# The rotary stage of a four-layer network on one core: the last two feed-forward batches get banks and buffers of their own, the value projections stand earlier, one output product is cut in two

## What is computed

```
# attention: 16 query heads, 4 key/value heads of 128, 128 context + 128 own keys
q, k, v = x @ wq, x @ wk, x @ wv ;  kc, vc = ctx @ wk_ctx, ctx @ wv_ctx
q, k, kc = rms_norm(q), rms_norm(k), rms_norm(kc);  q, k = rope(q), rope(k)
probs = softmax(q @ concat(kc, k).T / sqrt(128) + causal)     # 128 x 256 per head
x = x + tanh(g) * (probs @ concat(vc, v)) @ wo                # wo: 2048 x 256
# feed-forward with quantised rows (127 levels, per row) and ternary weights, hidden 1024
h = silu(quant(norm(x)) @ gate_w.T + gate_b) * (quant(norm(x)) @ val_w.T + val_b)
x = x + tanh(g') * (quant(h) @ out_w.T + out_b)
```

## Time and profile before

| | us |
|---|---|
| median of 3 runs (lowest, highest) | 2508.88 (2505.51, 2517.94) |
| the profiled execution | 2485.77 |
| its span in the trace | 2483.6 |
| mean granted TensorE clock, share of full | 0.952 |
| busy in the span: TensorE, VectorE, ScalarE, GpSimd | 2174.7, 1512.0, 1125.3, 745.6 |

### The profile page before, as it was taken

The page is one execution under the profiler, slowest core; times in us unless marked ns, Lnnn a source line. Parts: engine busy times, 40 slices in busy tenths (PEclk is TensorE's granted clock), DMA queues, the critical chain, the costliest instruction groups (busy, mean ns, idle before and its releaser), DMA issues. The chain is left out here.

```text
span 2483.6 us, 38366 instructions
## 1 busy us (share of the span) xinstructions
PE 2174.7 (88%) x10438; PEld 1376.0 (55%) x10486; DVE 1512.0 (61%) x3702; ACT 1125.3 (45%) x3555; POOL 745.6 (30%) x932
## 2 busy tenths in 40 slices
PE   6969999988888688879999999999995788869999
PEld 3446677756455344435556656665653444445685
DVE  6975434456455577765676777677765577753244
ACT  2021244411455355545565556555552477742242
POOL 5705500056233200023344444344433100003104
PEclk9969999999999899999999999999997699979999
DMA  6902245453200000000000000000000000201143
GB/s 218 300 21 85 91 136 161 147 163 114 118 1 0 3 1 0 0 26 1 1 1 1 0 0 0 0 0 0 0 0 1 5 5 4 84 24 42 61 134 100
DMA packets 85587, 127.18 MB, mean 51 GB/s; under 512 B 12418, under 2 KB 74626, under 8 KB 84226
## 3 DMA queue, kind: packets, MB, share of 16 engines
q1 hardware_dynamic: 75490, 98.52, 12.5%
q0 software_dynamic: 9984, 27.28, 3.5%
HBM read 91.41 MB, written 47.84 MB: 56 GB/s over the span
## 5 line engine op out<-in xcount | busy, mean ns | idle before, releaser
L2371 ACT ACTIVATE l2x_prob<-l2x_pS,l2x_nb,l2x_rms_q 128x256 f32<-128x256 f32 x256 | 142.5, 565 | 116.5 <-DVE l2x_nb L2606 114.7
L1035 ACT ACTIVATE moe_act_g<-moe_pG 128x96 f32<-128x96 f32 (+1 forms) x159 | 53.2, 335 | 267.2 <-PE moe_pU L968 186.9
L1186 PE MATMUL l2x_pQ<-big,l2x_xT 128*128 128x512 f32 x312 | 149.6, 602 | 4.7 <-DVE l2x_part L2584 4.3
L2603 DVE TENSOR_REDUCE l2x_negmax<-l2x_pS 128x2 f32<-128x512 f32 x128 | 87.7, 685 | 92.5 <-PE l2x_pS L2191 89.7
L928 POOL DMA_INDIRECT moe_yk<-route_y,moe_slot_i x72 | 71.1, 987 | 218.9 <-DMA route_y<-moe_y 188.5
L3113 DVE TENSOR_TENSOR l3f_hid<-l3f_act_g,l3f_pA 128x256 f32<-128x256 f32 (+1 forms) x103 | 38.1, 370 | 159.0 <-ACT l3f_act_g L3024 117.6
L2201 PE MATMUL l2x_pOT<-l2x_probT,l2x_v 128*128 128x512 f32 x256 | 124.7, 610 | 4.5 <-ACT l2x_probT L2386 4.5
L2191 PE MATMUL l2x_pS<-l2x_kT,l2x_qT 128*128 128x256 f32 x512 | 128.3, 380 | 0.0
L2937 PE MATMUL l3f_pA<-big,l3f_xnT 128*128 128x512 f32 x256 | 125.4, 614 | 0.0
L2210 PE MATMUL l2x_pT<-big,l2x_oT 128*128 128x256 f32 x512 | 121.1, 379 | 0.7 <-ACT l2x_oT L2379 0.7
L1515 ACT ACTIVATE l1f_ex<-l1f_pS,l1f_negmax 128x128 f32<-128x128 f32 x256 | 73.0, 368 | 104.0 <-DVE l1f_negmax L1546 104.0
(11 more groups left out here) (498 smaller groups left out, 5753.1 us busy)
## 6 DMA issues: line engine op xcount, KB each, us to landing
route_x<-in_c_zero SPq DMA_DIRECT2D x1, 13184.0 KB, 81.6
moe_xg<-route_x SPq DMA_DIRECT2D x103, 128.0 KB, 2.2
route_y<-moe_y SPq DMA_DIRECT2D x103, 128.0 KB, 1.7
big<-in_e_gu SPq DMA_DIRECT2D x1, 6144.0 KB, 19.0
l3f_xg<-route_x SPq DMA_DIRECT2D x39, 128.0 KB, 2.2
route_y<-l3f_y SPq DMA_DIRECT2D x39, 128.0 KB, 1.7
big<-in_f_gu SPq DMA_DIRECT2D x1, 4096.0 KB, 12.2
big<-in_e_down SPq DMA_DIRECT2D x1, 3072.0 KB, 25.0
```

The lines of the kernel that those rows point to most:

```text
L1186: last = pe.matmul(out, lhsT=xT[:, k, :], rhs=w[:, k, cols], start=(k == 0), stop=(k == KC - 1))
L2371: ins = act.activation(prob[g % 2][:, h, :], pS[j][:, (h % 2) * 2 * P:(h % 2 + 1) * 2 * P], ACT.Exp, scale=rms_q[g][:, h:h + 1], bias=nb[: ...
L2603: dve.tensor_reduce(negmax[:, c], pS[j][:].rearrange("p (h k) -> p h k", h=2), AX.X, ALU.max, negate=True).then_inc(S["max_steps"], 1)
```

## The change

1. TensorE and ScalarE: `value_rows` of x moves from the end of slot 3 (and of the prologue) to slot 0 of its own batch, that of the context from the end of slot 0 to slot 1. Both now stand right behind `proj` (TensorE) and `squares` (ScalarE).
2. TensorE: in slot 3 `output` is cut into heads 0 and 1 before the second `turn_probs`, and heads 2 and 3 behind it.
3. The last batch has its own feed-forward rows, in attention buffers that are free by then (`prob`, `probT`, `qT`, `krows`). The four `f_up` products of the last two batches go to pQ, pTq, pS0, pS1; the turn of x of batch 15 goes to pP, the turn of h and output product of batch 14 to pOT. Their waits follow these buffers.
4. `finish` is written out anew on each engine: the products of batch 14 stand between the last attention steps. The rounding of the hidden rows of batches 14 and 15 goes from GpSimd to ScalarE.

```diff
+        f_rows = (f_gate, f_val, f_th[:], f_xqT[:], f_qh_q[:], f_hqT)
+        f_rows_last = (prob[0][:].rearrange("p h k -> p (h k)"), prob[1][:].rearrange("p h k -> p (h k)"),
+                       probT[:].rearrange("p a h t -> p (a h t)"),
...
+        def up_bank(c, n):
+            return (pQ, pTq, pS[0], pS[1])[n] if is_last(c, 2) else pF
+
+        def turn_bank(c, what):
+            return {("x", B - 1): pP, ("h", B - 2): pOT}.get((what, c), pF) if isinstance(c, int) else pF
...
+            def output_first(b, p, g):
                 pe.wait_ge(S["ot_read"], 4 * b + g + 1)
                 after(pe, S["added"], 4 * b + g)
...
+                output_heads(g, (0, 1))
...
+            def output_second(b, p, g):
+                output_heads(g, (2, 3)).then_inc(S["out_ps"], 1)
...
@@ TensorE, slot
                     proj(b, p, g + 4)
                 elif not last:
                     proj(b + 1, 1 - p, 1 if g == 2 else 3)
+                if g < 2:
+                    value_rows(b, p, 1 - g)
                 if g == 3:
+                    output_first(*before(b, p, g, 2))
                     turn_probs(*before(b, p, g, 1), 1)
-                if at_least(b, g, 2):
+                    output_second(*before(b, p, g, 2))
+                elif at_least(b, g, 2):
...
-                if g == 0:
-                    value_rows(b, p, 0)
...
                     if g == 3:
                         trans(b + 1, 1 - p, 2)
-                        value_rows(b + 1, 1 - p, 1)
@@ TensorE, finish
+                f_up(B - 2, 0)
+                f_up(B - 2, 1)
                 turn_probs(B - 1, 1, 3, 0)
                 turn_probs(B - 1, 1, 3, 1)
                 output(B - 1, 1, 2)
                 values(B - 1, 1, 3, 2 * B)
+                f_up(B - 2, 2)
+                f_up(B - 2, 3)
                 output(B - 1, 1, 3)
-                for b in (B, B + 1):
-                    for g in range(4):
-                        f_first(b, g)
-                        f_second(b, g)
+                f_turn_h(B - 3)
+                f_out(B - 3)
+                f_turn_x(B - 1)
+                for n in range(4):
+                    f_up(B - 1, n)
+                f_turn_h(B - 2)
+                f_out(B - 2)
                 f_turn_h(B - 1)
                 f_out(B - 1)
@@ ScalarE, finish (behind probs, probs, values)
+                f_tanh(B - 2, 0)
+                f_h_turned(B - 3)
+                f_tanh(B - 2, 1)
+                f_x_turned(B - 1)
+                f_quant_h(B - 2)
+                f_tanh(B - 1, 0)
+                f_h_turned(B - 2)
+                f_tanh(B - 1, 1)
+                f_quant_h(B - 1)
                 f_h_turned(B - 1)
@@ ScalarE, new
+            def f_quant_h(c):
+                act.wait_ge(F["qh_steps"], 4 * c + 4)
+                if not is_last(c):
+                    act.wait_ge(F["hq_ps"], c)
+                act.activation(f_set(c)[4], f_set(c)[1], ACT.Copy, bias=-ROUND).then_inc(F["qh_ready"], 1)
@@ GpSimd, finish
+                f_quant_h(B - 3)
+                f_product(B - 2, 0)
+                fm.pool(pool, B - 1, 1)
+                f_product(B - 2, 1)
+                f_bias(B - 1)
+                f_product(B - 1, 0)
+                f_product(B - 1, 1)
@@ VectorE, finish
                 add_out(B - 1, 1, 2)
+                f_evict(B - 2, 0, 0)
+                f_evict(B - 2, 0, 1)
                 add_out(B - 1, 1, 3)
+                f_stats(B - 1, 1)
+                f_evict(B - 2, 0, 2)
+                f_evict(B - 2, 0, 3)
+                fm.normalise(dve, B - 1, 1)
+                f_quant_x(B - 1, 1)
+                f_hidden(B - 2, 0)
+                f_add(B - 3, 1)
+                f_hidden(B - 2, 1)
+                f_quant_h(B - 2, 0)
+                for n in range(4):
+                    f_evict(B - 1, 1, n)
+                f_hidden(B - 1, 0)
+                f_hidden(B - 1, 1)
+                f_quant_h(B - 1, 1)
+                f_add(B - 2, 0)
                 f_add(B - 1, 1)
```

More of the change, by code:

```diff
@@ L2204, in values, with output_heads, output @@
                 last.then_inc(S["ot_ps"], 1)
-            def output(b, p, g):
+            def output_heads(g, hs):
+                for h in hs:
+                    last = pe.matmul(pT[:, C:2 * C], lhsT=oT[:, h, :], rhs=W["l2_wo"][:, 4 * g + h, :],
+                                     start=(h == 0), stop=(h == 3))
+                return last
+            def output_first(b, p, g):
                 pe.wait_ge(S["ot_read"], 4 * b + g + 1)
                 after(pe, S["added"], 4 * b + g)
[L2209 to L2212, removed]
+                output_heads(g, (0, 1))
+            def output_second(b, p, g):
+                output_heads(g, (2, 3)).then_inc(S["out_ps"], 1)
+            def output(b, p, g):
+                output_first(b, p, g)
+                output_second(b, p, g)
             def turn_probs(b, p, g, j):
@@ L2227, in f_turn_x @@
                     pe.wait_ge(F["gv_read"], 4)
-                after(pe, F["added"], c - 1)
+                if is_last(c):
+                    pe.wait_ge(S["pT_read"], 8 * B)
+                else:
+                    after(pe, F["added"], c - 1)
                 for k in range(KC):
-                    last = pe.transpose(pF[:].bitcast(BF16)[:, k * P:(k + 1) * P], f_qx_q[:, k * P:(k + 1) * P],
+                    last = pe.transpose(turn_bank(c, "x")[:].bitcast(BF16)[:, k * P:(k + 1) * P], f_qx_q[:, k * P:(k + 1) * P],
                                         G["identb"][:])
@@ L2242, in f_up @@
                 w = W["l2f_gate_q"] if n % 2 == 0 else W["l2f_val_q"]
-                project(pe, pF[:], f_xqT, w, half(n // 2)).then_inc(F["gv_ps"], 1)
+                project(pe, up_bank(c, n)[:], f_set(c)[3], w, half(n // 2)).then_inc(F["gv_ps"], 1)
             def f_turn_h(c):
                 pe.wait_ge(F["qh_ready"], c + 1)
-                if isinstance(c, int) and c == B - 1:
-                    pe.wait_ge(F["added"], B - 1)
+                if is_last(c):
+                    pe.wait_ge(F["added"], B - 2)
+                elif is_last(c, 2):
+                    pe.wait_ge(S["ot_read"], 4 * B)
+                elif is_last(c, 3):
+                    pe.wait_ge(F["xqT_ready"], c + 2)
                 else:
@@ L2257, in f_out @@
                 pe.wait_ge(F["hqT_ready"], c + 1)
-                if not (isinstance(c, int) and c == B - 1):
+                if not is_last(c, 3):
                     pe.wait_ge(F["gv_read"], 4 * c + 8)
                 for t in range(HT):
-                    last = pe.matmul(pF[:, 0:C], lhsT=f_hqT[:, t, :], rhs=W["l2f_out_q"][:, t, :], start=(t == 0),
+                    last = pe.matmul(turn_bank(c, "h")[:, 0:C], lhsT=f_set(c)[5][:, t, :], rhs=W["l2f_out_q"][:, t, :], start=(t == 0),
                                      stop=(t == HT - 1))
@@ L2660, in f_evict @@
                 j = n // 2
[L2661 removed]
+                rows, dst = (f_gate_b, f_val_b)[n % 2], f_set(c)[n % 2]
                 if n == 0:
                     dve.wait_ge(F["scale_ready"], 2 * c + 1)
[L2664 removed]
+                if n == 1 and not is_last(c):
                     after(dve, F["qh_ready"], c)
                 dve.wait_ge(F["gv_ps"], 4 * c + n + 1)
[L2667 removed]
+                dve.scalar_tensor_tensor(dst[:, half(j)], up_bank(c, n)[:], f_step[p][:, n % 2:n % 2 + 1], rows[:, half(j)],
                                          ALU.mult, ALU.add).then_inc(F["gv_read"], 1)
```

68 lines of the change are left out of this document (34 added, 34 removed).

## The result

| | before | after |
|---|---|---|
| median, us (lowest, highest; 4 runs each) | 2507.20 (2503.89, 2517.94) | 2481.36 (2479.43, 2487.56) |
| ratio, 95% interval | | 0.9898 (0.9874 to 0.9923) |
| profiled execution, us | 2485.77 | 2483.09 |
| span, us | 2483.6 | 2481.2 |

A forecast was written before the change was run, and what follows sets the result against it. TensorE was taken to bound the rotary stage, no engine the drain. Stage -8.5 and drain -15.9 sum to -24.4 us, taking the median 2508.88 to 2484.5, rounded 2485 us; range 2468 to 2500.

The forecast's parts named there:

- 15 passes of the slots: Rotary stage: slots 0, 1 and 3 together give -0.57 us per batch, -8.5 us over 15.
- batch 0's rest with the prologue: Stage start: prologue loses one projection, slot 0 then waits for VectorE's normalised rows; near 0, bounds 0 and -1.7 us.
- the drain: After the last slot's first scores: ends at 1911.4 instead of 1927.3, -15.9 us, bounds -12 and -18.
- The three terms: Value projections moved forward, per batch: slot 0 -1.01 us, slot 1 +1.71, slot 3 -1.27.
- Rival 1: Rotary stage: the probT and oT waits go with nothing in their place, 2.2 us a batch; 2460 us; chance 0.09.
- the halving: Slot 3's output product: 0.86 us fills a wait but returns before the value product; 0, bounds 0 and 0.86 a batch.
- quantising of x of batch 15: VectorE in the drain: 1.9 us, between the clean 1.5 and 2.2 beside GpSimd.
- My reading of it: Drain, exclusive port lock of VectorE and GpSimd: loss could be one product more, drain -14.8, sum 1.1 us smaller.
- rival 3: TensorE clock behind the drain: denser drain holds 2.4 GHz, saving up to 6 us; 2478 us; chance 0.07.
- Rival 4: Slot 3: new idle places bring the clock down each batch, +75 us less 24; 2560 us; chance 0.02.
- rival 2: Slots 0 and 1: value-row copy delays the second probability copy, so only the drain gains; 2493 us; chance 0.17.
- rival 5: Drain: other banks and buffers remove no wait, only the rounding gets shorter; 2500 us; chance 0.03.

The follow-up runs named there:

- split_alone: The kernel before with only the output product of slot 3 halved: slot 3 13.13 us, batch 49.20 us, drain 54.88 us.
- drain_alone: The kernel before with only the new drain (parts 3 and 4 of the change): batch 49.21 us, drain 41.22 us.
- gpsimd_rounds: The changed kernel with the drain's rounding of hidden rows of batches 14 and 15 back on GpSimd: drain 43.93 us.
- probs_first: The changed kernel with x's value projection put back and ScalarE's second probability copy before its squares in slot 3: batch 48.19 us, ratio 0.9863 to the kernel before.
- early_normalise: As probs_first, with VectorE normalising the next batch's x in slot 0 before its rotary products: batch 47.57 us, stage 792.23 us, ratio 0.9850 to the kernel before.

## Why the prediction was right, and where it was off

**The sum.** Forecast -24.4 us, 2485 us; measured -25.8 by the medians, -25.16 in the stage's trace, 2481.36 us. The range held it. By terms, forecast and measured: 15 passes of the slots -8.5 and -8.48, batch 0's rest with the prologue 0 and -1.35, the drain -15.9 and -15.33. That the sum is off by only 0.8 us is partly luck: two errors of 1.35 and 0.57 us have opposite signs, and about 0.9 of the first is scatter. Of the 3.6 us between 2485 and 2481.36, 1.7 come from the median of before, which a fourth execution moved from 2508.88 to 2507.20.

**The slots.** The three terms were -1.01, +1.71, -1.27 for slots 0, 1 and 3; measured -1.01, +1.72, -1.26. What made this work is that each was a difference of start times in one timeline, with the new end of a step set by the copy that it must wait for, not by the wait that was removed. Rival 1, which subtracted the waits of the earlier trace rows, would have had 2.2 us a batch; 0.54 came. `split_alone` shows the same for the halving, taken at 0.

**The prologue.** Taken near 0, with -1.7 as the far bound. The prologue was 2.22 us shorter in the first profile; but the same prologue in `drain_alone`, which is that of the kernel before, took 15.94 and not 16.87, so about 0.9 of the 2.2 is scatter. Slots 0 and 1 of batch 0, which the term takes in, lost 0.87 us (7.60 and 9.99 to 7.76 and 10.70). So the term measured -1.35, within its bounds, or about -0.4 without the scatter.

**The stage.** From the first scores to the last slot it was -7.61 us. This holds the 0.87 us that slots 0 and 1 of batch 0 lost; the 15 passes of slot 3 (batches 0 to 14) and of slots 0 and 1 (batches 1 to 15) are -8.48, as forecast.

**The drain.** Forecast 40.1 (1871.32 to 1911.4), measured 40.62. The chain is the one described. Its steps, counted from the last slot's start, forecast and measured: last `add_out` 18.1 and 17.9; first eviction of batch 15 26.9 and 27.2; batch 15 rounded on VectorE 34.2 and 34.8; end 40.1 and 40.6.

```profile
1899.03 0.48 DVE L2688 SCALAR_TENSOR_TENSOR x_all<-l2x_pT,tg,x_all 128x256 f32<-128x256 f32 x1 [2.60 <-PE l2x_pT L2227]
...
1909.78 2.58 POOL L2553 TENSOR_TENSOR l2x_prob<-l2x_prob 128x512 f32<-128x512 f32 x2 [5.94 <-DVE l2x_prob L2732]
...
1911.16 2.35 DVE L2739 SCALAR_TENSOR_TENSOR l2x_probT<-l2x_probT,l2x_prob 128x512 f32<-128x512 f32 x2
...
1916.02 1.06 ACT L2464 ACTIVATE l2x_krows<-l2x_prob 128x1024 bf16<-128x1024 f32 x1 [4.29 <-DVE l2x_prob L2755]
...
1921.28 0.48 DVE L2762 SCALAR_TENSOR_TENSOR x_all<-l2x_pF,l2x_f_scale,x_all 128x256 f32<-128x256 f32 x1 [4.91 <-PE l2x_pF L2305]
```

The missing half microsecond is made of small terms. From the last `add_out` to the first eviction of batch 15 it was 9.3 us for 8.8, of which 0.2 in the add and 0.3 in the quantising of x beside GpSimd (next paragraph). The second hidden half ended 0.3 us later against the evictions than forecast; the two halves took 2.35 us one behind the other (1911.16 to 1913.51), beside GpSimd's second product. The evictions added 0.1; the last `add_out` and the final chain gave 0.2 and 0.1 back. ScalarE's rounding, which the trace of before did not show, took 1.06 us; I had taken 1.03 as its time goes with the columns. The Trainium skill (ScalarE: Activation LUTs, "What ACT_TABLE_LOAD costs") has 186 ns and 0.833 ns per column for an instruction with immediate scale and bias, 1.04 us here; the row agrees.

**GpSimd beside VectorE.** The quantising of x of batch 15 was taken as 1.9 us, between 1.5 alone and 2.2 beside GpSimd. It was 2.16, from the peak at 1902.07 to the hidden half at 1904.23, so the upper end was right.

```profile
1902.07 0.42 DVE L2708 TENSOR_REDUCE l2x_f_peak<-l2x_f_xn 128x1 f32<-128x256 f32 x1
...
1903.09 0.89 DVE L2719 TENSOR_SCALAR small<-l2x_f_xn,l2x_f_inv 128x256 f32<-128x256 f32 x1
...
1903.11 0.72 POOL L2566 TENSOR_TENSOR x_all<-x_all,small 128x256 f32<-128x256 f32 x1
...
1904.23 0.68 DVE L2739 SCALAR_TENSOR_TENSOR l2x_f_th<-l2x_f_th,small 128x512 f32<-128x512 f32 x1
```

The rounding took 0.89 us, as in the earlier trace rows. What stands beside it is not the product of 128x512 but GpSimd's addition behind it, 0.72 us. So it is in the earlier trace rows too: the product shown there ended at 1897.92, 0.06 us after the rounding began, and the addition ran from 1897.88. The rule of the Trainium skill that I weighed (SBUF — State Buffer, "SBUF: two separate sides") has the pair held for a whole instruction. The trace doesn't contradict it: the rounding lost 0.54 us beside an addition of 0.72. My reading of it, one product more and a drain 1.1 us longer than by the rows, did not come: the drain was 0.5 above the rows' sum and 0.6 below that one.

**The clock (rival 3).** In the drain it was 0.84 instead of 0.69, and in the 32.73 us behind it 0.63 instead of 0.55. Yet the next stage's first scores came 23.2 us after its start in both. Nor is the higher clock behind the drain clearly the denser drain's: `split_alone`, with the old drain, had 0.61 there, `gpsimd_rounds` and `probs_first`, with the new one, 0.54 and 0.58. The drain's own length doesn't hang on it either: in the seven profiles of this drain the granted clock went from 0.77 to 0.88, and its length stayed within 0.02 us. Rival 4 is refuted by the 1.00 of the first line above.

**Rivals 2 and 5.** The copy of value rows costs nothing in the batches of the loop; doubled, it cost 0.5 us in batch 0 alone. And the drain alone gives 14.7 us.

## What to carry to other kernels

The wait that a profile names is not what its removal is worth: ask what the waiting instruction, or the one moved away, had been covering. Here moving two like projections out of two like waits was worth 1.02 us a batch for one and cost 0.46 to 0.49 for the other, and only start-to-start times at the old place, with the next copy's end as the new limit, told which. Filling one wait of a slot helps only if the engine that ends the next one is early as well; `early_normalise` needed a changed order on three engines to turn 0.85 us into a gain. And where whole executions scatter by more than the change, compare the stage with itself.

## What the runs showed of the hardware

- In 13 profiles the unchanged code behind the stage took 556 to 567 us, and the first turn of the rotary stage came between 1091.9 and 1120.2 us; slots of the stage and the drain repeat within 0.02 us between kernels that share them.
- Where what follows the stage took 566 us and not 559, the granted TensorE clock over its first 100 us was 0.74 and not 0.79 to 0.84, with the same instructions.
- A wait of TensorE that the view names as 0.59 us cost 0.85 us from start to start: the next instruction no longer starts 0.16 us before the end of the one ahead, and takes 0.11 us longer to its successor.
- A normalisation of 128x256 on VectorE took 0.41 us ahead of GpSimd's addition of 128x512 rows and 1.20 us beside it. The order within a slot is worth that much on VectorE alone.
- A rounding of 128x1024 rows to bf16 takes 1.06 us on ScalarE and 2.78 us on GpSimd.
